# One expert tile fewer, the first four weight loads placed ahead of a wait, and an activation table loaded early, in a two-block model kernel on one core

## The reference, cut to what matters

```python
logits = t @ gate_w + gate_b
top_v, top_i = jax.lax.top_k(logits, K)            # K = 2, E = 8
probs = jax.nn.softmax(top_v, axis=-1)
def body(acc, ew):
    w1, b1, w2, b2, we = ew
    h = _swiglu(t @ w1 + b1)                        # 128 -> 512 -> 256
    y = h @ w2 + b2                                 # 256 -> 128
    return (acc + we[:, None] * y, None)
...
x = x + gb * (x + y)                                # the block's gated sum
```

## Time and profile before

| | us |
|---|---|
| median of 3 runs | 981.67 (980.34 to 982.22) |
| the profiled execution, its own time | 986.01 |
| its span, first to last instruction | 984.1 |
| mean granted TensorE clock in the span | 0.916 |

### The profile page before, as it was taken

One profiled execution on the slowest core, in us unless ns is written; L12 is line 12 of the kernel. 1 busy time (PEld: TensorE's weight loads), 2 busy tenths in 40 slices (PEclk: granted clock), 3 DMA queues, 4 the chain that ended last, 5 costly groups with the idle time before them and its releaser, 6 DMA issues.

```text
span 984.1 us, 23471 instructions
## 1 busy us (share of the span) xinstructions
PE 839.7 (85%) x7426; PEld 649.8 (66%) x7441; DVE 775.3 (79%) x2069; ACT 658.5 (67%) x1737; POOL 562.5 (57%) x573
## 2 busy tenths in 40 slices
PE   6978891699999939999999999998306999999991
PEld 5945570354445428888888888887105889889880
DVE  2988678899998766779999999999753666666996
ACT  3557127899995375667777787764605888888880
POOL 1211007747873325343888888888772666666773
PEclk9989795699999969999999999999557999999996
DMA  5330262233233121000111111111125655555977
GB/s 149 91 92 1 87 174 61 97 130 114 98 129 114 60 45 46 2 1 21 37 35 37 35 45 37 34 37 42 47 94 157 221 182 178 183 182 187 338 247 252
DMA packets 83813, 101.31 MB, mean 103 GB/s; under 512 B 15390, under 2 KB 65497, under 8 KB 81516
## 3 DMA queue, kind: packets, MB, share of 16 engines
q1 hardware_dynamic: 71100, 79.46, 25.5%
q0 software_dynamic: 8704, 18.11, 5.3%
q10 hardware_dynamic: 3888, 2.25, 0.7%
HBM read 76.11 MB, written 23.67 MB: 101 GB/s over the span
## 4 chain that ended last, share of the span: by engine, by line
PE 52%; DVE 3%; DMA 3%; issue 2%; POOL 1%; ACT 1%; SPq 1%; ACTq 0%; POOLq 0%; DVEq 0%
PE ps L2494 13%; PE ps L2251 11%; PE ps L2515 6%; PE ps L2267 3%; PE ps L2329 2%; PE ps L2242 2%; PE ps L2477 2%; PE ps L2213 2%; PE ps L2388 2%; PE ps L2368 2%; PE ps L2262 2%; PE ps L2228 1%; POOL rows_of L1524 1%; PE ps L2316 1%; DMA parts<-gx,dest 1%
## 5 line engine op out<-in xcount | busy, mean ns | idle before, releaser
L1524 POOL DMA_INDIRECT rows_of<-payb,posu x128 | 146.1, 1141 | 40.6 <-issue 27.1
L1515 POOL TENSOR_TENSOR kvb<-qk,v 128x1024 f32<-128x1024 f32 x64 | 126.1, 1975 | 75.0 <-DVE qk L1889 50.3
L1115 PE MATMUL ps<-masked,ew 128*128 128x512 f32 x256 | 130.0, 623 | 4.1 <-DVE masked L1043 3.5
L2251 PE MATMUL ps<-con,kvb 128*128 128x128 f32 x1024 | 126.0, 276 | 0.0
L2251 PEld LDWEIGHTS ps<-con,kvb 128*128 128x128 f32 x1024 | 119.4, 192 | 1.0 <-issue 1.0
L2176 DVE TENSOR_SCALAR qk<-ps,b 128x256 f32<-128x256 f32 x144 | 62.9, 478 | 69.7 <-PE ps L2494 67.1
L1549 POOL DMA_INDIRECT parts<-h,dest x72 | 71.0, 986 | 52.5 <-ACT h L1791 38.5
L1043 DVE TENSOR_TENSOR masked<-f_t,wide 128x512 f32<-128x512 f32 x128 | 88.3, 707 | 9.8 <-PE ps L1115 9.5
L1865 DVE TENSOR_TENSOR qc<-ps,qk 128x1024 f32<-128x1024 f32 x64 | 78.1, 1220 | 18.4 <-PE ps L2251 17.8
L1549 POOL DMA_INDIRECT parts<-gx,dest x72 | 73.6, 1023 | 32.6 <-issue 17.4
L2515 PE MATMUL ps<-w,f_t 128*128 x576 | 76.1, 275 | 0.0
(11 more groups left out here) (347 smaller groups left out, 2133.5 us busy)
## 6 DMA issues: line engine op xcount, KB each, us to landing
wide<-hot_dram SPq DMA_DIRECT2D x16, 1024.0 KB, 4.6
kvb<-rows_of SPq DMA_DIRECT2D x72, 132.0 KB, 2.5
ex<-in_w_dram SPq DMA_DIRECT2D x36, 256.0 KB, 2.8
lg<-in_w_dram SPq DMA_DIRECT2D x36, 256.0 KB, 2.8
toep<-taps_dram SPq DMA_DIRECT2D x16, 512.0 KB, 5.8
xg<-parts SPq DMA_DIRECT2D x16, 512.0 KB, 5.6
x_tok<-in_x_dram SPq DMA_DIRECT2D x16, 256.0 KB, 2.8
rows<-rows_dram SPq DMA_DIRECT2D x16, 192.0 KB, 3.1
```

The lines of the kernel that those rows point to most:

```text
L1115: nc.tensor.matmul(ps[:, w % 2, :], ew0[:, e, :], masked[e % 4][:, :], start=False, stop=(e == E - 1)).then_inc(s["product"], 1)
L1515: nc.gpsimd.tensor_tensor(kv[g % KB][:, :, :].rearrange("p e (h d) -> p e h d", h=H), k_in, v_in, ALU.mult).then_inc(s["kv"], 1)
L1524: nc.gpsimd.indirect_dma_start(rows_of, bass.IndirectOffsetOnAxis(ap=posu[w % 2][:, slot, t:t + 1], axis=0), pay[w % PB][:, t, :], None).t ...
L2251: last = nc.tensor.matmul(cum(g)[:, e, :], kv[g % KB][:, e, :], k("upto"), start=True, stop=True)
```

## The change

It has three parts.

1. RUN = 71 tiles are run. The buffers keep the size for 72. The 72nd tile's loads, products, activation and sends are left out, and the waits count 71 uses of each ring.
2. SP waits for the plan (`place`) first, reads `packs` and issues the weights of tiles 0 to 3, and then waits for the sends. In the loop, tiles 0 to 3 load their rows only.
3. ACT loads the table set for the experts right after its part of the padding rows, ahead of its wait for the plan.

```diff
--- before.py
+++ after.py
@@ -1164,6 +1164,10 @@
         E3 = 3 * E
         BT = -(-(2 * TILES // S + E - 1) // V) * V
         NP = BT // V
+        RUN = 2 * TILES // S + E - 1
+
+        def uses(j, ring):
+            return len(range(j, RUN, ring))
         parts = nc.dram_tensor("parts", [(2 * TILES + S * BT) * P, D], F32).ap()
         number = sb("number", [P, BT])
         cnt = sb("cnt", [P, E])
@@ -1327,7 +1331,7 @@
                     return self.made[per, k]
 
                 def exists(self, v):
-                    return not isinstance(self.i, int) or 0 <= self.i * V + v < BT
+                    return not isinstance(self.i, int) or 0 <= self.i * V + v < RUN
 
                 def done(self, name, v, alone=False):
                     if self.exists(v):
@@ -1429,8 +1433,6 @@
                     sp.wait_ge(s["pads"], 16 * E)
                     sp.wait_ge(s["experts"], (1 + NF) * 16)
 
-                    for j in range(PB):
-                        sp.wait_ge(s_scat[j], 16 * SCATTERS * (B // PB))
                     sp.wait_ge(s["place"], 2)
                     need(sp, "tri", B * C)
                     need(sp, "pay_ps", B)
@@ -1438,6 +1440,16 @@
                     need(sp, "sub", B)
                     need(sp, "ln", B)
                     need(sp, "qk", B)
+
+                    def load_w1(t, packed, v):
+                        e = t.expert(packed, v)
+                        sp.dma_start(w1c[v % WC], a["w1"][:, bass.ds(e, 1), :].rearrange("p e i -> p (e i)")).then_inc(s_w1[v % WC], 16)
+                    begin = Tiles(sp, 0)
+                    packed0 = begin.packed()
+                    for v in range(WC):
+                        load_w1(begin, packed0, v)
+                    for j in range(PB):
+                        sp.wait_ge(s_scat[j], 16 * SCATTERS * (B // PB))
 
                     both = parts[0:2 * TILES * P, :].rearrange("(b p c j) d -> p b (c j d)", p=P, c=C, j=2)
 
@@ -1455,8 +1467,10 @@
                         sp.dma_start(out[b].rearrange("(c p) d -> p c d", p=P), x_tok[:, b * C:(b + 1) * C, :]).then_inc(s_done, 16)
 
                     def body(t, steps):
-                        packed = t.packed() if t.exists(0) else None
+                        packed = packed0 if t.i == 0 else t.packed() if t.exists(0) else None
                         for v in steps:
+                            if not t.exists(v):
+                                continue
                             early = t.i * V + v - AT - V - 3
                             if early == 0:
                                 complete(AT)
@@ -1466,17 +1480,17 @@
                             t.done("x_ps", v - V, alone=True)
                             t.grouped("dest", v - V, alone=True)
                             sp.dma_start(xt[:, v, :, :], rows_of[bass.ds(at, SP), :].rearrange("(p c) d -> p c d", c=S)).then_inc(s_in[v], 16)
-                            e = t.expert(packed, v)
-                            t.done("h_ps", v - WC)
-                            sp.dma_start(w1c[v % WC], a["w1"][:, bass.ds(e, 1), :].rearrange("p e i -> p (e i)")).then_inc(s_w1[v % WC], 16)
+                            if t.exists(v - WC):
+                                t.done("h_ps", v - WC)
+                                load_w1(t, packed, v)
                         if isinstance(t.i, int) and t.i == 0:
                             sp.dma_start(gates[:, :, :], rows_dram[:, 4 * D:5 * D].partition_broadcast(P)).then_inc(s_gate, 16)
                     passes(sp, body)
                     sp.wait_ge(m["weights"], 16)
                     for v in range(V):
-                        sp.wait_ge(s_in[v], 16 * NP)
+                        sp.wait_ge(s_in[v], 16 * uses(v, V))
                     for j in range(WC):
-                        sp.wait_ge(s_w1[j], 16 * (BT // WC))
+                        sp.wait_ge(s_w1[j], 16 * uses(j, WC))
                     for b in range(BW - Q):
                         store(b)
                     complete(BT_EARLY)
@@ -1485,7 +1499,7 @@
                     for b in range(BW - Q, AW):
                         store(b)
                     for v in range(V):
-                        sp.wait_ge(s_out[v], 16 * S * NP)
+                        sp.wait_ge(s_out[v], 16 * S * uses(v, V))
                     for b in range(BW, B):
                         load_parts(b)
                     for q in range(Q):
@@ -1550,7 +1564,7 @@
                                                                  yw[u][:, c, :], None).then_inc(s_out[u], 16)
                     passes(pool, body, back=LAG)
                     for v in range(V):
-                        pool.wait_ge(s_out[v], 16 * S * NP)
+                        pool.wait_ge(s_out[v], 16 * S * uses(v, V))
 
                 @block.scalar
                 def _(act):
@@ -1748,6 +1762,7 @@
                     for e in range(E // 2, E):
                         row = act.value_load(counts[0:1, e:e + 1], min_val=e * CAP, max_val=(e + 1) * CAP - SP)
                         act.dma_start(rows_of[bass.ds(row, SP), :].rearrange("(p c) d -> p c d", c=S), far[:, :, :]).then_inc(s["pads"], 16)
+                    nc.scalar.preload_act_table_set("gelu_apprx_sigmoid_and_others")
                     act.wait_ge(s["place"], 2)
                     act.wait_ge(s["weights"], 3 * 16)
                     need(act, "den", B)
@@ -2496,7 +2511,7 @@
                                     if f == 1:
                                         last.then_inc(m["hg_ps"], 1)
                                 last.then_inc(m["h_ps"], 1)
-                            if v == 0 and t.exists(-1):
+                            if v == 0 and t.exists(-2):
                                 before = t.packed(-1)
                             if v == 1 and t.exists(0):
                                 packed = t.packed()
```

## The result

The changed kernel took 975.9 us (median of 4 runs, 975.13 to 976.25), against 981.9 in the runs of the kernel before beside it. The ratio is 0.9931, 95% interval 0.9914 to 0.9948: faster by 6.8 us, or 5.1 to 8.4. The forecast was 977.0, a gain of 4.6 us by its sum, with a range of 975.5 to 979.2, that is a gain of 6.2 to 2.5. Two more comparisons came later, with ratios 0.9950 and 0.9942; the three ratios have a mean of 0.9941, which is 5.8 us, and their intervals overlap. Over all 17 runs the changed kernel has a median of 976.3 and a mean of 977.0; the kernel before has 981.7 and 982.1 over 82 runs, which gives 5.4 and 5.1. So the gain is some 5 to 6 us. The direction and the steps held, but the terms of the sum were too small; and the first two profiles, which differ by 10.8 us, show more than the change gives.

What follows compares the result with a forecast made beforehand. PE was taken to bound the middle tiles, the wait for the last routing send the front, and POOL's last sends the tail. Gains 2.78 + 1.6 + 0.22 = 4.6 us took 981.67 to 977.1, said as 977.0; range 975.5 to 979.2.

Steps and rivals of the forecast that it cites:

- POOL's slot: Tail: with 71 tiles POOL loses two sends, so its last send starts 2.78 us earlier.
- the landing of tile 1's rows: Front: with no weights beside them, tile 1's rows land perhaps 0.1 us sooner.
- the landing of the last send: Tail: time from POOL's last send to its arrival, 4.26 us before, taken to keep its length.
- 71 tiles, the sends: Tail: dropping the 72nd tile gains 2.78 us through POOL's last sends, not PE's 2.94; ends 1.5 and 4.2.
- 71 tiles, the landing: Tail: the last send's arrival might be slower (gain 1.53) or quicker (gain 4.24); no change was taken.
- the earlier stores: Tail: SP's stores and the loads of parts behind them start 2.94 us earlier, in less full time.
- the closer stores of ACT: Tail: ACT's final stores come nearer the last load of parts and may lengthen its 3.62 us by 0.8.
- The landing eats the tail: Rival: tile 70's send lands as slowly as tile 68's, 5.51 us; tail gain 1.53, time 978.3; chance 0.12.
- Weights ahead: Front: first four weight loads issued before the wait for sends; tile 0's first product 1.6 us earlier, sends not slowed.
- The clock: Front: PE's clock rise follows the work, full 1.6 us; rival, it keeps its place, 0.8, time 977.9, chance 0.15.
- The table: Front: loading ACT's table in idle time hides 1.28 us, but PE gains only 0.22.
- The sum: Whole kernel: 2.78 + 1.6 + 0.22 = 4.6 us gained, from 981.67 to 977.1, said as 977.0.

Runs made afterwards that it cites:

- the late stores: Changed kernel, but SP holds its first six stores and what stands behind them until PE has turned tile 70; 979.0 us, ratio 0.9973.
- extra products: Changed kernel plus 44 unused PE products ahead of tile 0: 974.1 us; with the table at its old place 975.4; 48, 3 between turns and stores moved ahead: 973.0.
- the early stores: Changed kernel, but SP issues its first six stores ahead of the waits for rows and weights to land; 975.5 us, ratio 0.9945.
- the kernel before again: The kernel before the change, run and profiled once more with no edit; ratio 1.0004, profiled execution's own time 988.18 us.

## Why the prediction was right or wrong, step by step

- **Which step failed.** No wait, path or overlap that I named was wrong. What failed is the size of the terms: POOL's slot (2.78, measured 3.1) and, in the front, the landing of tile 1's rows (0.1 sooner, measured 0.3 in the first two profiles and 0.6 between the means). I also set the landing of the last send at no change; it fell by 1.2 in the first two profiles and by 0.5 in the means, which isn't clear of the spread. Together the stretches give 5.75 where the sum had 4.6.
- **71 tiles, the sends.** The place was right: POOL's last two sends, with PE long through. The term was mis-sized: 2.78 was read off one pair of sends, while over the profiles the last send moves by 3.1. The 2.94 that PE spends on a tile would have been the nearer reading; why it is 3.1 isn't shown.
- **71 tiles, the landing.** I named the earlier stores as a gain, set the closer stores of ACT against them, and took nothing. I overlooked that the last send comes earlier by as much as the stores do. The stretch fell from 4.27 to 3.74 in the means, with overlapping values, and its cause is open. The loss that I set against it, a longer last load, shows as 3.83 against 3.62 in the two first profiles, and as 0.05 in the mean of the stretch to the end.
- **The landing eats the tail.** That rival was wrong for this kernel: it took tile 68's 5.51 us for that of the last send, which landed in 3.10 to 4.18 in the three profiles of the changed kernel. With the late stores, 5.86, it would have been right.
- **Weights ahead.** The steps held: SP back with time to spare, rows issued 0.94 earlier, tile 1's rows 1.6, sends of 0.96 us. The size was low: rows that travel with no weights beside them landed 0.3 faster (2.08 against 2.39), where I had 0.1, and the first product started 1.9 earlier, not 1.6. The row that I read was the fastest of its kind: over all profiles the landing shortens by 0.6, and the product starts 2.2 earlier. Between the means of all profiles without extra products the front shortens by 2.15 (38.6 to 36.4), where parts 2 and 3 together had 1.82.
- **The clock.** That its rise follows the work on average, and not in each execution, agrees with the fronts: in the kernel before alone they were 37.9 and 39.5. Of these 1.6 us, 0.5 is the slower landing of tile 1's rows; the rest is the low clock, under which the products of tiles 0 and 1 took 3.41 and 2.52 us against 3.10 and 1.73. The Trainium skill (TensorE: Matmul & The Clock Gate, Part 1) says that the chip's watch on PE isn't tied to the kernel; by that the clock's rise falls at different places against the work, and the traces agree: the kernel before ran tile 1's product at the high clock in one profile and mostly at the low one in the other.
- **The table.** 0.22 was read rightly from one row, but it isn't a constant: it was 0 in three profiles, 0.5 in one and 0.75 with the clock up ahead of tile 0. It was never the 1.28 of the load. Part 3 by itself was not run; the times can't tell it from nothing.
- **The sum.** 4.6 against 5.1 to 5.8 over all runs; the stretches of the profiles add up to 2.15 + 3.1 + 0.5 = 5.75. The first comparison's 6.8 is 1 us above that, inside its own interval. The 5.5 us that the first two profiles differ by ahead of the last routing send are spread of the first stage. I treated a median of three runs and one profile as if they didn't have it. The range was also narrow at its fast end: my own ends, 4.2, 1.9 and 0.22, add up to 6.32 and 975.35, and I wrote 975.5.

## What to carry to other kernels

When an engine is through long before the end, work that is taken off it is worth what it takes off the engine that is late. Where the last transfer lands among bulk stores, look for the wait that gates the first of them: here the landing went with how far ahead of the last send they begin, so a change that moves both by the same amount need not help. A wait that is satisfied late should have nothing behind it that could have been issued ahead. What is issued ahead is also no longer beside the transfers that must follow, and those land sooner. Before a gain of half a per cent is put down to a change, cut two or more profiles of the same kernel into stretches, and see how far they differ where nothing was changed.

## What the runs showed of the hardware

- The same kernel reached the same instruction 6.5 us apart in two executions (734.0 and 740.5). Of it 6.0 are there within the first 50 us: the first products at L485 start at 7.1 or 8.8 us, behind an activation that waited for a load until 5.20 or 6.92, and from 20 to 30 us PE, busy throughout, had a granted clock of 1.00 in one and 0.66 in the other.
- The clock can fall while PE has work: after 12 us of unbroken products and two waits of 1.1 and 0.8 us it fell in one execution as the next products began, and in another, with waits of 0.8 and 0.7, it stayed.
- An indirect send's landing depends on what is beside it. For the same bytes it took 2.37 us with the early stores, at a DMA share of 0.71 while it was under way, 3.10 in the changed kernel at 0.91, and 5.86 with the late stores, at 1.13. The share alone doesn't give it: the kernel before again had 4.56 at 0.81.
- A tile's rows, 132 KB, landed in 2.39 to 2.89 us with a weight load beside them and in 2.03 to 2.15 without.
